# One quad in sixteen of the scan's product with C moved from GpSimd to VectorE, in every group

## What is computed

```python
delta = softplus(einsum('blr,er->ble', dt, dt_proj_w) + dt_proj_b)
dA = exp(delta[..., None] * -exp(A_log))             # decay, per channel e (512) and state n (16)
BX = delta[..., None] * Bm[:, :, None, :] * xc[..., None]
# h[t] = dA[t] * h[t-1] + BX[t]                      # the scan over the 1024 rows
y = einsum('blen,bln->ble', hs, Cm) + D * xc         # product with C, summed over n
out = einsum('ble,de->bld', y * silu(z), out_proj_w)
```

## Time and profile before

| | |
|---|---|
| median of 3 runs | 3230.02 us (3225.7 to 3231.91) |
| profiled execution | 3228.74 us, of it 3226.9 us from the first to the last instruction |
| mean granted TensorE clock | 0.947 of full |
| PE / DVE / ACT / POOL busy | 2898.2 / 2482.5 / 2391.9 / 2642.7 us |
| products with C on GpSimd | 480 of 2365 ns |
| products with C on VectorE | 64 of 686 ns (one tile; GpSimd's are of two) |

### The profile page before, as it was taken

How to read it: one execution, slowest core, us unless ns; L and a number is a source line. 1 busy time by engine, 2 the same in 40 slices (tenths; PEclk the granted TensorE clock), 3 DMA queues, 4 the chain that set the end, 5 groups by cost and what they waited for, 6 DMA issues and landing times.

```text
span 3226.9 us, 54604 instructions
## 1 busy us (share of the span) xinstructions
PE 2898.2 (90%) x17328; PEld 1833.4 (57%) x17328; DVE 2482.5 (77%) x5644; ACT 2391.9 (74%) x5299; POOL 2642.7 (82%) x1590
## 2 busy tenths in 40 slices
PE   5898888899999999999999999999999999988567
PEld 3565455475665656566565656656565655654246
DVE  3256978788787878879787887878787887879980
ACT  4587868787786878778687878878687787855432
POOL 1117999998998989999899989989998998988870
PEclk9999999899999999999999999999999999989788
DMA  3004453446445454644545364444545454455531
GB/s 82 14 35 144 145 164 111 158 146 206 131 143 173 153 182 140 205 145 147 184 127 198 127 210 141 169 153 149 190 128 197 149 179 140 151 182 180 176 124 41
DMA packets 285967, 477.31 MB, mean 148 GB/s; under 512 B 38451, under 2 KB 93363, under 8 KB 285683
## 3 DMA queue, kind: packets, MB, share of 16 engines
q1 hardware_dynamic: 285682, 473.83, 44.7%
HBM read 388.79 MB, written 84.93 MB: 147 GB/s over the span
## 4 chain that ended last, share of the span: by engine, by line
PE 70%; POOL 9%; ACT 8%; issue 6%; DVE 5%; DMA 2%; SPq 1%; ACTq 0%; DVEq 0%; POOLq 0%
PE bank L518 21%; PE bank L526 9%; PE bank L641 7%; PE bank L777 6%; PE bank L763 6%; PE bank L563 6%; PE bank L551 6%; PE bank L716 5%; POOL h_rows L1539 4%; POOL h_rows L1549 4%; PE bank L579 3%; ACT prob L832 2%; PE bank L512 2%; ACT zb L797 2%; DVE h_rows L1315 1%
## 5 line engine op out<-in xcount | busy, mean ns | idle before, releaser
L1539 POOL TENSOR_TENSOR h_rows<-u_rows,b_rows 128x1024 f32<-128x1024 f32 x512 | 1203.3, 2365 | 35.1 <-DMA b_rows<-bc_dram 34.4
L1549 POOL TENSOR_TENSOR h_rows<-h_rows,c_rows 128x1024 f32<-128x1024 f32 x480 | 1129.6, 2365 | 63.7 <-DVE state L1322 49.1
L1003 ACT ACTIVATE bank<-d_rows,a_rep 128x512 f32<-128x512 f32 x1024 | 682.5, 688 | 154.4 <-DMA d_rows<-delta_dram 44.3
L1315 DVE TENSOR_TENSOR_SCAN h_rows<-bank,state,h_rows 128x512 f32<-128x512 f32 x480 | 594.5, 1267 | 44.9 <-ACT bank L1003 30.1
L1315 DVE TENSOR_TENSOR_SCAN h_rows<-bank,h_rows 128x512 f32<-128x512 f32 x480 | 575.0, 1213 | 51.2 <-ACT bank L1003 40.0
L832 ACT ACTIVATE prob<-prob,neg_max 128x256 f32<-128x256 f32 x1024 | 509.4, 504 | 85.9 <-DVE neg_max L1098 85.8
L1098 DVE CUSTOM_DVE_ANT_0 prob<-bank,bands 128x256 f32<-128x256 f32 x896 | 335.9, 417 | 166.3 <-PE bank L551 162.4
L563 PE MATMUL bank<-ident,prob 128*128 128x128 f32 x2048 | 316.1, 281 | 61.3 <-ACT prob L832 55.1
L563 PEld LDWEIGHTS bank<-ident,prob 128*128 128x128 f32 x2048 | 235.8, 142 | 218.9 <-issue 199.7
L716 PE MATMUL bank<-h_rows,sum_n 128*32 128x512 f32 x2048 | 281.6, 625 | 70.7 <-POOL h_rows L1549 58.2
L518 PE MATMUL bank<-nb,w 128*128 128x512 f32 x512 | 270.7, 685 | 15.8 <-ACT nb L790 12.0
(11 more groups left out here) (164 smaller groups left out, 4847.8 us busy)
## 6 DMA issues: line engine op xcount, KB each, us to landing
u_rows<-u_dram SPq DMA_DIRECT2D x256, 256.0 KB, 3.9
d_rows<-delta_dram SPq DMA_DIRECT2D x256, 256.0 KB, 4.1
b_rows<-bc_dram SPq DMA_DIRECT2D x256, 256.0 KB, 3.1
c_rows<-bc_dram SPq DMA_DIRECT2D x256, 256.0 KB, 3.1
w<-in_W SPq DMA_DIRECT2D x28, 1024.0 KB, 7.1
zs_dram<-region_b SPq DMA_DIRECT2D x64, 256.0 KB, 2.8
xc_dram<-region_b SPq DMA_DIRECT2D x64, 256.0 KB, 3.5
u_dram<-region_b SPq DMA_DIRECT2D x64, 256.0 KB, 2.1
```

Of the source, the lines that this page charges most:

```text
L1003: e.activation(banks[at.bank][:, :], d_rows[:, c, :], ACT.Exp, scale=a_rep[:, k:k + 1]).then_inc(filled[at.bank], 1)
L1315: e.tensor_tensor_scan(rows, banks[at.bank][:, :], rows, start, ALU.mult, ALU.add).then_inc(drained[at.bank], 1)
L1539: e.tensor_tensor(half_of(i, b, half), u_rows[:, 2 * half:2 * half + 2, :], twice(b_rows[:, b % 2, :]), ALU.mult).then_inc(bx_ready.sem, 1)
L1549: e.tensor_tensor(rows, rows, twice(c_rows[:, b % 2, :]), ALU.mult).then_inc(hc_ready.sem, 1)
```

## The change

`vector_out` becomes `vector_quads`: in groups 14 and 15 the odd quads as before, and in every other group quad 9 alone. Its four tiles then go the way that is described above for the last groups. The tiles of that quad give their banks back one step later (`uses_of`), and the semaphore counts are now worked out from lists of quads. The list of steps is the same, entry by entry; which number of bank a tile gets differs in most places.

```diff
-def vector_out(i, b, batches):
-
-    return i >= 2 * batches - 2 and b % 2 == 1
+MIDDLE_QUADS, LAST_QUADS = (9,), tuple(range(1, QUADS, 2))
+
+def vector_quads(i, batches):
+
+    return LAST_QUADS if i >= 2 * batches - 2 else MIDDLE_QUADS
...
-        return ([(f"d{k}", SCAN0 + 2 * k + DECAY_AT, SCAN0 + 2 * k + (1 if shared and k // 4 % 2 else 0))
+        return ([(f"d{k}", SCAN0 + 2 * k + DECAY_AT, SCAN0 + 2 * k + (1 if k // 4 in quads else 0))
...
         def out_formed(i, b):
 
-            last = 2 * BATCH - 2
-            if vector_out(i, b, BATCH):
-                return hc_by_vector.at(i - last, b // 2 + 1)
-            done = last * 2 * QUADS + (i - last) * QUADS + b + 2 if i >= last else 2 * (i * QUADS + b + 1)
-            return hc_ready.sem, CREDIT + done
+            if by_vector(i, b):
+                return hc_by_vector.sem, CREDIT + quads_by["vector"].index((i, b)) + 1
+            return hc_ready.sem, CREDIT + 2 * quads_by["gpsimd"].index((i, b)) + 2
...
-                if vector_out(i, k // 4, BATCH):
+                if by_vector(i, k // 4):
                     e.tensor_tensor_scan(banks[at.bank][:, :], banks[at.bank][:, :], rows, start,
...
-                e.wait_ge(*h_in_bank.at(i - 2 * BATCH + 2, n + 1))
+                e.wait_ge(h_in_bank.sem, CREDIT + 4 * quads_by["vector"].index((i, b)) + k % 4 + 1)
...
-                    if b is not None and not vector_out(i, b, BATCH):
+                    if b is not None and not by_vector(i, b):
                         times_c(b, half)
```

More of the change, by code:

```diff
@@ L110, with uses_of @@
 )
-def vector_out(i, b, batches):
-    return i >= 2 * batches - 2 and b % 2 == 1
-def uses_of(stage, shared=False):
+MIDDLE_QUADS, LAST_QUADS = (9,), tuple(range(1, QUADS, 2))
+def vector_quads(i, batches):
+    return LAST_QUADS if i >= 2 * batches - 2 else MIDDLE_QUADS
+def uses_of(stage, quads=()):
     if stage == "attention":
@@ L179, in schedule @@
     for stage in PLACES:
-        for shared in (False, True):
-            for name, first, last in uses_of(stage, shared):
-                begins.setdefault((stage, shared, first), []).append(name)
-                ends.setdefault((stage, shared, last), []).append(name)
+        for quads in ({(), MIDDLE_QUADS, LAST_QUADS} if stage == "scan" else {()}):
+            for name, first, last in uses_of(stage, quads):
+                begins.setdefault((stage, quads, first), []).append(name)
+                ends.setdefault((stage, quads, last), []).append(name)
     def earlier(thread, i):
@@ L196, in schedule @@
             _, _, stage, i, step = chain[0]
-            shared = stage == "scan" and vector_out(i, 1, batches)
-            names = begins.get((stage, shared, step), ())
+            quads = vector_quads(i, batches) if stage == "scan" else ()
+            names = begins.get((stage, quads, step), ())
             if len(names) <= len(idle) and not any(c in chains for c in earlier(*key)):
@@ L208, in schedule @@
             signalled[bank] += not (stage == "scan" and name[0] == "y")
-        for name in ends.get((stage, shared, step), ()):
+        for name in ends.get((stage, quads, step), ()):
             idle.append(uses[stage, i, name].bank)
@@ L455, in states_kept, with by_vector @@
             return state_ready.sem, CREDIT + (i // 2) * 2 * QUADS + (2 * QUADS if i % 2 else 2 * b + half + 1)
-        def out_formed(i, b):
-            last = 2 * BATCH - 2
-            if vector_out(i, b, BATCH):
-                return hc_by_vector.at(i - last, b // 2 + 1)
-            done = last * 2 * QUADS + (i - last) * QUADS + b + 2 if i >= last else 2 * (i * QUADS + b + 1)
-            return hc_ready.sem, CREDIT + done
+        quads_by = {"vector": [], "gpsimd": []}
+        for i in range(2 * BATCH):
+            for b in range(QUADS):
+                quads_by["vector" if b in vector_quads(i, BATCH) else "gpsimd"].append((i, b))
+        def by_vector(i, b):
+            return b in vector_quads(i, BATCH)
+        def out_formed(i, b):
+            if by_vector(i, b):
+                return hc_by_vector.sem, CREDIT + quads_by["vector"].index((i, b)) + 1
+            return hc_ready.sem, CREDIT + 2 * quads_by["gpsimd"].index((i, b)) + 2
         def fetched_again(i):
@@ L1319, in keep_states @@
                 k = 4 * b + 2 * half
-                if not vector_out(i, b, BATCH):
+                if not by_vector(i, b):
                     e.wait_ge(*gone(use(f"d{k + 1}")))
@@ L1324, in times_c @@
             def times_c(k):
-                at, b, n = use(f"d{k}"), k // 4, k // 8 * 4 + k % 4
-                e.wait_ge(*h_in_bank.at(i - 2 * BATCH + 2, n + 1))
+                at, b = use(f"d{k}"), k // 4
+                e.wait_ge(h_in_bank.sem, CREDIT + 4 * quads_by["vector"].index((i, b)) + k % 4 + 1)
                 if k % 4 == 0:
@@ L1353, in dve_scan @@
                 k = tile_at(step, 1)
-                if k is not None and vector_out(i, k // 4, BATCH):
+                if k is not None and by_vector(i, k // 4):
                     times_c(k)
```

## The result

The changed kernel takes 3248.55 us (median of five runs, 3245.09 to 3256.96) against 3230.02 us: a ratio of 1.0067, 95% interval 1.0048 to 1.0086. Every ratio here leaves out executions in the slow state, of which there was one, of 9889.59 us in `e9_quad_1`. The kernel before has five executions by now too, with the same median and range.

The account below looks back on a forecast made before the run. TensorE was taken to bound the middle groups. 3228.74 us + 16.8 (groups 2 to 13) + 2 (groups 0 and 1) = 3247.5; the median running 1.3 us above that execution, the forecast was 3248.5 us, range 3234 to 3264.

Parts of the forecast that it names:

- What bounds the kernel: TensorE holds 70% of the chain of waits; in the twelve middle groups, relieving GpSimd gains 0.
- The cost on VectorE: Quad 9's products on VectorE: tiles follow at 1.93 us, and the scan behind the quad waits another 0.24 us.
- The new wait: Groups 2 to 13: scores s24 on TensorE wait about 1.4 us for d39's bank, freed 2.85 us later.
- Groups 0 and 1: The first two groups, GpSimd on the chain: +2 us for both, bounds -9.5 and +6 us.
- the three marks: Group 1: no TensorE wait at quad 9's sums; GpSimd waits for VectorE at quad 11's second product, 1.0 us later.
- So the 1.4 us pass into the group's length.: Groups 2 to 13: TensorE's work behind the scores is back to back, so 12 x 1.4 us = 16.8 us.
- No later detour gives them back.: Groups 2 to 13: later detours begin with a TensorE matmul, so none recovers the 1.4 us.
- What was costed at nothing behind the wait: ScalarE's decay of d40 and VectorE's masks, 1.2 and 2.2 us later: cost nothing, at most 0.8 us a group.
- The main rival: TensorE's clock falls to half behind each new wait, 1.7 us each, 12 times: 3269 us; chance 0.12.
- A milder form, by some us either way: Longer groups move TensorE's existing stretches at half clock, changing the time by some us either way.
- The row that I set against the rival: A TensorE wait of 1.14 us, said to stand alone, followed by 107 us at a granted clock of 1.00.
- GpSimd's idle time behind quad 9: GpSimd was to stand idle for some 6 us behind quad 9 in the profile after.

Follow-up runs that it names:

- e9_quad_1: The same change made to quad 1 instead of quad 9 in groups 0 to 13, against the kernel before: 3250.90 us, ratio 1.0066.
- e4_no_product: The kernel before with GpSimd's product of quad 9 cut to 128x2 elements in groups 0 to 13, nothing added on VectorE: 3231.36 us, ratio 0.9996.
- e11_pe_3: The kernel before with the first matmul of scores s24 made three times more in groups 2 to 13: 3245.64 us, ratio 1.0047.
- e12_pe_16: The kernel before with the first matmul of scores s24 made 16 times more in groups 2 to 13: 3368.36 us, ratio 1.0430.
- e3_groups_0_1: The change made in groups 0 and 1 alone, against the kernel before: 3233.56 us, ratio 1.0012.
- e7_banks_and_add: The changed kernel with idle banks handed out in another order and VectorE's add into x3 ahead of d39's scan: 3247.51 us, ratio 1.0045 to the kernel before.
- e1_other_bank: The changed kernel with idle banks reordered in groups 2 to 13, so s25 gets t4.0's bank, not d39's: 3253.65 us, ratio 1.0063 to the kernel before.
- e8_quad_6_groups_0_1: VectorE forms the product of quad 6, not 9, in groups 0 and 1 alone, against the kernel before: 3237.03 us, ratio 1.0013.

## Why the prediction was right, and where it was not

- **What bounds the kernel.** Right: TensorE waits as seldom for GpSimd as before, and `e4_no_product` puts GpSimd's relief at nothing.
- **The cost on VectorE.** Right: 120 products (64 of them in groups 14 and 15) of 677 to 693 ns, a pace of 1.93 us, a last product 0.21 us longer in its hand-over (0.24 in the earlier trace rows).
- **The new wait.** Right in place, cause and size: 1.40 to 1.43 us in each of the twelve groups.
- **Groups 0 and 1.** About right: +2 us forecast. At the scores behind group 1 the profiled execution is 2.2 us late (547.93, before 545.71), but the wait of 2.82 us that stood behind them is gone, and what is left at 598.57 is 1.2 us. One execution does not measure that: already at the scores of group 0, where no quad 9 has been reached, the profiled executions of kernels that are the same up to there (before, `e4_no_product`, `e11_pe_3`, `e12_pe_16`) lie between 83.6 and 86.1 us; `e3_groups_0_1` gives 0 to 8 us. In group 1 the three marks came out as said: the wait for quad 9's product is gone, and GpSimd and TensorE are 1.2 us late. The scores behind group 1, before and now, then GpSimd and TensorE:

```profile
545.71 1.71 PE L551 MATMUL bank<-kT,q_own 32*128 32x256 f32 x8 [0.19 <-DVE h_rows L1315]
...
547.93 2.07 PE L560 MATMUL bank<-kT,q_own 32*128 32x256 f32 x8 [1.40 <-DVE h_rows L1342]
...
573.16 2.39 POOL L1558 TENSOR_TENSOR h_rows<-h_rows,c_rows 128x1024 f32<-128x1024 f32 x1 [0.85 <-DVE h_rows L1324]
...
598.57 3.77 PE L535 MATMUL bank<-w_o,q_own 128*128 128x256 f32 x9 [4.02 <-POOL q_own L1462]
```

   What the first two rows say was not in the forecast: the scores wait in the first groups too, for VectorE's product of d38. They had waited 0.19 us for its scan before, so there was no slack.
- **"So the 1.4 us pass into the group's length."** Right for groups in which the clock falls at the same places (group 7: 1.28 us longer, with 1.43 us of wait in it), and `e11_pe_3` gives the same time with a delay of 1.28 us on TensorE alone. It is not the whole of the account. In the mean of ten groups there are +1.41 us at the scores, +0.53 us at the softmax, and 0.5 us less busy time, since 10.2 us of a group instead of 12.3 us are at half clock. That the last two cancel is not something I had worked out; over all twelve groups they do not quite, and it is 15.7 us instead of 16.8. The experiments that were to take the wait away did not settle it, since they left 0.8 us (`e7_banks_and_add`) or more (`e1_other_bank`) of the delay in place. The 0.6 us that `e7_banks_and_add` did take away brought back less than 0.1 us.
- **"No later detour gives them back."** A detour did not give time back, it took more: the softmax wait is 2.47 us in every group, where four of the ten had 1.1 to 1.2 us.
- **What was costed at nothing behind the wait.** Wrong as soon as the wait is gone: in `e1_other_bank` ScalarE waits 0.70 us and TensorE 0.41 us behind it. In the changed kernel the scores' own wait covers that.
- **The clock.** The main rival did not come true: no half clock follows the new wait in groups 2 to 13. "A milder form, by some us either way" did. The row that I set against the rival, 1616.72 with a wait of 1.14 us, was misread: that wait does not stand alone. It is short because a stretch at half clock lies right ahead of it. The other six softmax waits of the same ten groups, of 2.46 or 2.47 us, each had 3.4 us at half clock beginning within 1 us behind them, and they were the rows to weigh. The rule of the Trainium skill ("TensorE: Matmul & The Clock Gate", A second HAM failure mode: psum-queue depth-cycling) that I weighed there did hold for 2.0 and 2.6 us in about half of the cases.
- **GpSimd's idle time behind quad 9.** About 6 us in one piece was forecast. The next idle times are 0.62 and 3.27 us: some of the 4.7 us goes into a shorter queue and is spent in small pieces.

```profile
1671.92 2.35 POOL L1548 TENSOR_TENSOR h_rows<-u_rows,b_rows 128x1024 f32<-128x1024 f32 x1 [0.62 <-PE bank L725]
1677.55 0.29 POOL L1455 COPY rden_wide<-rden 128x128 f32<-128x128 f32 x1 [3.27 <-DVE rden L1120]
```

**What stays open.** How much a delay of less than 1.3 us costs. Set side by side, what TensorE was held up by in each group (from the starts of its matmuls) and what the mean group became longer by:

| kernel | held up by, us | group longer by, us |
|---|---|---|
| the changed kernel | 1.41 | 1.38 |
| `e11_pe_3` | 1.28 | 1.38 |
| `e9_quad_1` | 1.05 | 1.41 |
| `e7_banks_and_add` | 0.80 | 1.32 |

The two upper rows agree with a delay that adds up, the two lower ones do not: up to 0.5 us a group come on top. In those two kernels the groups with the short softmax wait are gone as well, and nothing smaller was run. That the place of the half-clock stretches is what ties these kernels to one length is argued from the traces, not shown by a run of its own. Open too is how the starts differ: in the first two groups the waits at the scores were 1.4 us in the changed kernel's profile and 2.2 and 3.4 us in that of `e3_groups_0_1`, with the same instructions.

## What to carry to other kernels

Relief for an engine that is 80% busy is worth what the waits for it show, here nothing; and what an added step costs is read from who waits for its buffer, here the scores on TensorE, to a tenth of a microsecond. In a kernel that repeats one group many times over, compare groups in which TensorE's clock falls at the same places: there the wait is found in full, while the mean over all mixes it with the clock. Read a delay from the starts of what follows it, not from a share of a row in which several matmuls overlap, and not from the marked idle time alone: a delay of 1.28 us had looked like 0.4 us that way, and one of 1.05 us like 0.36. An experiment that takes a cause away has to be read the same way, for how much of the delay it really took; and a forecast that hits the number does not show the cause.

## What the runs showed of the hardware

- A stretch at half clock costs by its place: ahead of a wait of 2.47 us it shortened that wait to 1.14 us and cost little, right behind it it cost its full loss.
- The lengths of two successive groups together lie close to a few values, in different kernels: 372.1 us in the kernel before (1478.63 to 1850.77), in `e4_no_product` and in `e8_quad_6_groups_0_1`, 375.5 us in the changed kernel (1485.34 to 1860.79), in `e7_banks_and_add` and in `e9_quad_1`.
- Waits of TensorE of 1.4 us at the scores were followed by half clock in none of 12 groups, waits of 2.0 us in five and waits of 2.6 us in six.
- Some 5 us (4.8 to 5.3) of matmuls on 32 rows, with no gap between them, were followed by 10.2 us at half clock in each of twelve groups.
- The same float32 matmul of 32x256 made three times more held TensorE for 1.28 us, where four different ones behind each other took 1.07 us.
- A product of VectorE with both inputs in SBUF took up to 2.86 us beside GpSimd (median 1.75 us for the second product of a pair), with one of them in a PSUM bank at most 0.693 us.
